# Attention on TensorE in row bands of 32: scores in bands 0 and 1, maxima in bands 2 and 3, keys and queries kept twice

## What is computed

```python
q = split_heads(layernorm(x) @ Wq + bq)          # 8 heads of 4 numbers, 2048 queries
k = split_heads(ctx @ Wk + bk)                   # 1601 keys
v = split_heads(ctx @ Wv + bv)
attn = softmax(q @ k.T / sqrt(32))               # 8 x 2048 x 1601
x = x + tanh(g_xattn) * (merge_heads(attn @ v) @ Wo + bo)
xf = layernorm(x)
scores = softmax(xf @ router_w + router_b)       # 8 experts
G, idx = top_k(scores.T, 512)                    # each expert takes its 512 best tokens
eo = relu(xf[idx] @ w1 + b1) @ w2 + b2
x = x + tanh(g_ffn) * scatter_add(eo * G)
```

## Time and profile before

| | before |
|---|---|
| median of 3 runs (lowest, highest) | 595.6 us (595.19, 595.64) |
| profiled execution: its time | 594.75 us |
| profiled execution: its span | 592.9 us |
| TensorE matmul busy | 551.4 us, 93% |
| VectorE busy | 444.1 us, 75% |
| ScalarE busy | 397.4 us, 67% |

### The profile page before, as it was taken

How to read it: one execution, slowest core, us unless ns; L and a number is a source line. 1 busy time by engine, 2 the same in 40 slices (tenths; PEclk the granted TensorE clock), 3 DMA queues, 4 the chain that set the end, 5 groups by cost and what they waited for, 6 DMA issues and landing times.

```text
span 592.9 us, 12821 instructions
## 1 busy us (share of the span) xinstructions
PE 551.4 (93%) x5043; PEld 318.6 (54%) x5043; DVE 444.1 (75%) x811; ACT 397.4 (67%) x774; POOL 196.8 (33%) x193
## 2 busy tenths in 40 slices
PE   6798899998999989999999998899999999999994
PEld 4433333333333333333333344469889898898974
DVE  3889879996798967989897258746767868677541
ACT  2587789987888878898888830044665646655651
POOL 3058030024420063400158010240735626346234
PEclk9999999999999999999999999999999999999998
DMA  8600000000000000000000004122735556356133
GB/s 280 241 2 1 1 1 3 2 1 38 2 36 2 2 37 1 37 2 1 37 38 2 36 19 140 34 60 72 163 112 117 144 136 148 108 107 163 16 36 35
DMA packets 23807, 35.80 MB, mean 60 GB/s; under 512 B 3459, under 2 KB 16196, under 8 KB 23620
## 3 DMA queue, kind: packets, MB, share of 16 engines
q1 hardware_dynamic: 17604, 26.59, 13.8%
q0 software_dynamic: 6144, 8.39, 8.3%
HBM read 26.59 MB, written 8.39 MB: 59 GB/s over the span
## 4 chain that ended last, share of the span: by engine, by line
PE 67%; DVE 18%; ACT 5%; issue 4%; POOL 3%; DMA 1%; POOLq 0%; ACTq 0%; DVEq 0%; SPq 0%
PE ps L1719 15%; PE ps L1726 15%; PE ps L1488 12%; DVE mquart L1016 11%; PE ps L1475 6%; PE ps L1454 6%; PE ps L1384 2%; ACT probs L741 2%; PE ps L1345 2%; POOL xn L528 2%; PE ps L1360 1%; PE ps L1697 1%; PE ps L1672 1%; ACT osb L641 1%; PE ps L1513 1%
## 5 line engine op out<-in xcount | busy, mean ns | idle before, releaser
L1016 DVE TENSOR_REDUCE mquart<-ps 128x2 f32<-128x802 f32 x256 | 241.9, 988 | 33.4 <-PE ps L1454 30.2
L741 ACT ACTIVATE probs<-ps 128x512 f32<-128x512 f32 (+1 forms) x416 | 222.9, 599 | 24.0 <-PE ps L1475 20.8
L1488 PE MATMUL ps<-probs,vp 128*32 128x256 f32 (+1 forms) x1664 | 132.7, 391 | 4.5 <-ACT osb L641 4.5
L1454 PE MATMUL ps<-kpad,qrows 64*128 64x401 bf16 x512 | 90.6, 337 | 3.7 <-DVE mquart L1016 3.1
L1475 PE MATMUL ps<-qfull,kpad 64*128 64x256 bf16 (+1 forms) x832 | 89.8, 272 | 2.8 <-ACT x L762 0.9
L1313 DVE TENSOR_TENSOR h1l<-hf,h1h 128x512 fp32r<-128x512 f32 x64 | 44.4, 693 | 56.0 <-ACT hf L868 56.0
L867 ACT ACTIVATE h1h<-ps,b1T 128x512 fp32r<-128x512 f32 x64 | 44.0, 687 | 53.8 <-PE ps L1719 53.6
L1726 PE MATMUL ps<-w2h,h1h 128*128 128x256 f32 x256 | 73.8, 288 | 2.2 <-DVE h1l L1313 1.5
L1726 PE MATMUL ps<-w2l,h1h 128*128 128x256 f32 x256 | 72.4, 283 | 0.0
L1726 PE MATMUL ps<-w2h,h1l 128*128 128x256 f32 x256 | 72.3, 283 | 0.0
L1475 PEld LDWEIGHTS ps<-qfull,kpad 64*128 64x128 bf16 (+1 forms) x832 | 38.9, 96 | 48.2 <-ACT probs L741 25.1
(11 more groups left out here) (198 smaller groups left out, 682.3 us busy)
## 6 DMA issues: line engine op xcount, KB each, us to landing
w1raw<-in_L_ffn_w SPq DMA_DIRECT2D x16, 512.0 KB, 4.6
w2raw<-in_L_ffn_w SPq DMA_DIRECT2D x16, 512.0 KB, 4.7
xs<-in_x SPq DMA_DIRECT2D x4, 512.0 KB, 7.7
ctx_sb<-in_ctx SPq DMA_DIRECT2D x3, 512.0 KB, 5.8
out<-xs SPq DMA_DIRECT2D x3, 512.0 KB, 2.6
x_rows<-x SPq DMA_DIRECT2D x3, 512.0 KB, 2.6
b2b<-in_L_ffn_b SPq DMA_DIRECT2D x1, 1024.0 KB, 11.1
out<-xs SPq DMA_DIRECT2D x2, 256.0 KB, 2.0
```

Source lines behind the costliest of these rows:

```text
L741: nc.scalar.activation(out_p, ps[0:w, next_bank(), :], ACT.Exp, scale=float(SCALE)).then_inc(s_ex, 1)
L1016: nc.vector.tensor_reduce(mquart[:, u % 2, t, a, :, kq], ps[:, b:b + 2, 0:MAXW], AX.X, ALU.max).then_inc(s_mr, 1)
L1454: last = mm(ps[:, bank + b, 0:MAXW], qrows[band(b), g, q:q + P], kpad[band(b), g, a, lo:lo + MAXW], start=True, stop=True)
L1488: last = mm(ps[32 * hh:32 * hh + 32, PV, 0:UW], vp[0:w, kt, g, hh, :], probs[0:w, step % PROBS, hh, :], start=(kt == 0), stop=(kt == NKT - 1))
```

## The change

Keys are no longer padded. `kbands` holds each head's keys once in its own 32 rows, and `kturned` holds the same with partitions 0 to 63 and 64 to 127 exchanged, by DMA from `kbands`. The queries of a chunk are copied the same way from partitions 0 to 63 to 64 to 127 of `qturned`. Each score matmul and each maximum matmul now has 32 rows: scores use partitions 0 to 31 and 32 to 63 (`score_band`), maxima 64 to 95 and 96 to 127 (`max_band`). `qfull` has two halves `v` on partitions 0 to 63: `v` 0 for the two heads that stand there, `v` 1 for the two that stand in the other half, with 64-column matmuls in `place_max` and a 64x512 copy in `q_full`. In a step the `v` 0 scores of both banks come first, then the first tile, then the `v` 1 scores, then the second tile. The heads stand on the partitions in another order (`place_of`), for which the weights are spread anew with ten copies in place of eighteen. The SyncE queue gets 16 transfers for the keys and 8 for the queries; the bias `b2b` and the first expert weights stand behind those of chunk 0, and the loop of the stores is written out.

```diff
-        kpad = ar("kpad", [P, NG, 2, KEYS], BF16)
+        kbands = ar("kbands", [P, NG, KEYS], BF16)
+        kturned = ar("kturned", [P, NG, KEYS], BF16)
...
+            def turn_keys(j, g):
+                lo, w = KB[j]
+                sp.wait_ge(s_rows, BLOCKS.index(("k", j, g)) + 1)
+                sp.dma_start(kturned[64:P, g, lo:lo + w], kbands[0:64, g, lo:lo + w]).then_inc(s_kup[g], 16)
+                sp.dma_start(kturned[0:64, g, lo:lo + w], kbands[64:P, g, lo:lo + w]).then_inc(s_kdown[g], 16)
+            def turn_queries(c, g):
+                sp.wait_ge(s_rows, rows_of(c, g))
+                if c > 1:
+                    sp.wait_ge(s_mm, TILES * (PER_CHUNK * (c - 2) + PARTS * (g + 1)))
+                sp.dma_start(qturned[64:P, g, c % 2, :], qrows[0:64, g, CW * c:CW * c + CW]).then_inc(s_qt[NG * (c % 2) + g], 16)
...
-                take(qfull[:, g, UW * h:UW * h + UW], ps[:, next_bank(), 0:UW], s_qf)
+                take(qfull[0:64, g, :, UW * h:UW * h + UW], ps[0:64, next_bank(), :].rearrange("p (v q) -> p v q", v=2), s_qf)
...
-                split(j, j % 2, w, 2, krows[:, j % 2, 0:w])
-                dve.wait_ge(s_rows, j + 1)
-                for b in range(2):
-                    last = nc.vector.tensor_scalar(kpad[:, 0, b, lo:lo + w], krows[:, j % 2, 0:w],
-                                                   cst[:, C_HEAD + b:C_HEAD + b + 1], None, ALU.mult)
-                last.then_inc(s_kpad0, 1)
+                split(j, j % 2, w, 2, kbands[:, 0, lo:lo + w])
...
                 for b in range(2):
-                    last = mm(ps[:, bank + b, 0:MAXW], qrows[band(b), g, q:q + P], kpad[band(b), g, a, lo:lo + MAXW], start=True, stop=True)
+                    rows = max_band(b)
+                    queries = qrows[rows, g, CW * c + q:CW * c + q + P] if a else qturned[rows, g, c % 2, q:q + P]
+                    keys = (kbands if a else kturned)[rows, g, lo:lo + MAXW]
+                    last = mm(ps[:, bank + b, 0:MAXW], queries, keys, start=True, stop=True)
...
-                mm(ps[:, bank, 0:UW], ident_bf[:, :], qrows[:, g, q:q + UW], start=True, stop=False, skip_group_check=True)
+                for v in range(2):
+                    mm(ps[0:64, bank, UW * v:UW * v + UW], ident_bf[:, 64 * v:64 * v + 64], qrows[:, g, q:q + UW],
+                       start=(v == 0), stop=False, skip_group_check=True)
...
                 for kt in range(NKT):
+                    first, second = score_bank(u, kt, 0), score_bank(u, kt, 1)
+                    scores(u, kt, 0, 0, first)
+                    scores(u, kt, 1, 0, second)
                     for n in range(tiles_by(u, 2 * kt - 1), tiles_by(u, 2 * kt)):
                         max_tile(n)
-                    scores(u, kt, 0)
-                    scores(u, kt, 1)
+                    scores(u, kt, 0, 1, first).then_inc(s_sc, 1)
+                    scores(u, kt, 1, 1, second).then_inc(s_sc, 1)
```

More of the change, by code:

```diff
@@ L338, in dve_bank, with score_band, max_band, place_of @@
             return 3 + 2 * (n % 2)
[L340 to L342 removed]
+        def score_band(p):
+            return slice(32 * p, 32 * p + 32)
+        def max_band(b):
+            return slice(64 + 32 * b, 64 + 32 * b + 32)
+        def place_of(head):
+            return 2 * (head % 2) + head // 2
         PLACE = 10
@@ L431, in _ @@
                 load_w2(0, half)
-            with sp.Fori(0, LAST) as c:
+            for g in range(NG):
+                turn_queries(1, g)
+            for c in range(LAST):
                 sp.wait_ge(s_x1, c + 1)
-                sp.dma_start(out_v[:, bass.ts(c, CT), :], xs[:, bass.ts(c, CT), :]).then_inc(s_out1, 16)
+                sp.dma_start(out_v[:, CT * c:CT * c + CT, :], xs[:, CT * c:CT * c + CT, :]).then_inc(s_out1, 16)
+                if c + 2 < NC:
+                    for g in range(NG):
+                        turn_queries(c + 2, g)
                 sp.wait_ge(s_x2, c + 1)
-                sp.dma_start(x2_v[:, bass.ts(c, CT), :], x2[:, :, :]).then_inc(s_x2st, 16)
+                sp.dma_start(x2_v[:, CT * c:CT * c + CT, :], x2[:, :, :]).then_inc(s_x2st, 16)
             for half in range(2):
@@ L907, in _, with heads @@
-            for j in range(2):
-                for g in range(NG):
-                    last = nc.vector.tensor_copy(
-                        bqkr[:, NG * j + g, :].rearrange("p (h j d) -> p h j d", h=HG, d=HD)[:, :, 0:6, :],
-                        bias_sb[:, 32 * j + 16 * g:32 * j + 16 * g + 16].rearrange("p (h d) -> p h d", d=HD).unsqueeze(2).to_broadcast([1, HG, 6, HD]))
+            def heads(a, x):
+                return a.rearrange("p n (y x d) -> p n y x d", x=2, d=HD)[:, :, :, x, :]
@@ new lines, in places @@
+            def places(a, x):
+                return a.rearrange("p n (x y j d) -> p n x y j d", x=2, y=2, d=HD)[:, :, x, :, :, :]
+            w_in, w_out = [t[:, :, :].rearrange("p k (g c) -> p (k g) c", g=NG) for t in (wk_sb, wq_sb, wv_sb)], [
+                t[:, :, :, :].rearrange("p k g r -> p (k g) r") for t in (wkr, wqr)]
+            b_in = bias_sb[:, :].rearrange("p (n c) -> p n c", c=16)
+            for x in range(2):
+                for src, dst in zip(w_in, w_out):
+                    nc.vector.tensor_copy(places(dst, x)[:, :, :, 0:6, :], heads(src, x).unsqueeze(3).to_broadcast([P, KD * NG, 2, 6, HD]))
+                nc.vector.tensor_copy(places(w_out[0], x)[:, :, :, 7, :], heads(w_in[2], x))
+                nc.vector.tensor_copy(places(bqkr[:, NG:2 * NG, :], x)[:, :, :, 7, :], heads(b_in[:, 2 * NG:3 * NG, :], x))
+                last = nc.vector.tensor_copy(places(bqkr[:, :, :], x)[:, :, :, 0:6, :],
+                                             heads(b_in, x)[:, 0:2 * NG].unsqueeze(3).to_broadcast([1, 2 * NG, 2, 6, HD]))
@@ L1462, in place_max, with scores, score_bank @@
                 bank = next_act((s_qf, u + 1))
-                mm(ps[:, bank, 0:UW], ident_bf[:, :], qrows[:, g, q:q + UW], start=True, stop=False, skip_group_check=True)
-                for t in range(UQ):
-                    last = mm(ps[:, bank, P * t:P * t + P], mparts[:, t, :, :].rearrange("p h r -> p (h r)"), ident_bf[:, :],
-                              start=False, stop=True, skip_group_check=True)
+                for v in range(2):
+                    mm(ps[0:64, bank, UW * v:UW * v + UW], ident_bf[:, 64 * v:64 * v + 64], qrows[:, g, q:q + UW],
+                       start=(v == 0), stop=False, skip_group_check=True)
+                    for t in range(UQ):
+                        last = mm(ps[0:64, bank, UW * v + P * t:UW * v + P * t + P], mparts[:, t, 2 * v:2 * v + 2, :].rearrange("p h r -> p (h r)"),
+                                  ident_bf[:, :], start=False, stop=True, skip_group_check=True)
                 last.then_inc(s_mpl, 1)
-            def scores(u, kt, p):
+            def scores(u, kt, p, v, bank):
                 c, g, h, r = unit(u)
                 w = kt_rows(kt)
-                bank = next_act((s_ex, 2 * (NKT * u + kt) + p + 1))
-                for b in range(2):
-                    last = mm(ps[0:w, bank, UW * b:UW * b + UW], kpad[band(p), g, b, P * kt:P * kt + w],
-                              qfull[band(p), g, UW * h:UW * h + UW], start=True, stop=True)
-                last.then_inc(s_sc, 1)
+                if (c, h, kt, p, v) == (0, 0, 0, 0, 1):
+                    pe.wait_ge(s_kdown[g], 64)
+                rows = score_band(p)
+                return mm(ps[0:w, bank, UW * v:UW * v + UW], (kturned if v else kbands)[rows, g, P * kt:P * kt + w],
+                          qfull[rows, g, v, UW * h:UW * h + UW], start=True, stop=True)
+            def score_bank(u, kt, p):
+                return next_act((s_ex, 2 * (NKT * u + kt) + p + 1))
             def pv(u, kt):
```

62 lines of the change are left out of this document (21 added, 41 removed).

## The result

The changed kernel takes 607.9 us (median of 4 runs, 605.33 to 614.90), the kernel before in the same comparison 595.4 (594.61 to 595.64): 1.020 times as long, interval 1.014 to 1.026. Faster by 7 us was forecast; it is slower by 12.5. The profiled execution took 605.59 us with a span of 603.8. Its granted clock was 0.987 of full; 605.33 us came at 0.987 as well, 610.16 at 0.979 and 614.90 at 0.967. The kernel before held 0.992 to 0.997 in all 52 runs beside the experiments.

What follows compares the result with a forecast made beforehand. TensorE was taken as nearest to full in most attention units, VectorE as the bound in units r=3. Gains of 4.0, 5.4 and 0.3 us less 2.4 for placing gave 587.4, or 588.3 us as median, range about 584 to 592.

Steps and rivals of the forecast that it cites:

- part 1: Attention steps, scores beside maxima: 22 two-tile steps gain 4.0 us, 30 steps with other work gain 5.4 us.
- one-tile step: Attention step with one maxima tile: 1.09 us on the chain before, to stay at about 1.07, no gain taken.
- the sum: Whole kernel: -4.0 - 5.4 + 2.4 - 0.3 = -7.3 us, on a profiled 594.75 us.
- Placing: Maxima placed with more columns streamed: 2.4 us on TensorE over 11 placements; ScalarE's copy grows from 386 to 598 ns.
- the prologue: Ahead of the attention: fewer padding copies gain 0.7 us, first placement and copy cost 0.22 + 0.21; together -0.3 us.
- two-tile step: Attention step with two maxima tiles: to fall from 1.24 to 1.06 us, 0.18 each, 22 counted, 4.0 us.
- a granted clock of 1.2 GHz in the attention: Sign that the prediction is wrong: TensorE's clock at 1.2 GHz, against full 2.4 GHz, somewhere in the attention.
- that rival: In attention steps, 32-row matmuls don't run beside one another, scores' second pair waits for the tile; +13 us, 609; chance 0.09.
- The maxima starve: Attention tile stands behind both score banks' wait, TensorE late by 0.17 us in some 65 steps; costs 11, 599; chance 0.13.
- its sign: The reduction's idle time on VectorE, 30.7 us over the attention before, grows.

Runs made afterwards that it cites:

- experiment 6: Changed kernel's order, but the second bank's wait moved behind the first bank's first score matmul; 604.7 us (598.55 to 606.79).
- Experiment 5: Bands of 32 rows and the old matmul order, but both banks' waits put ahead of everything in a step; 609.6 us (608.83 to 615.94).
- experiment 2: Changed kernel's bands of 32 rows, with the step order and waits of the kernel before; 595.3 us (591.88 to 603.43, 10 runs), ratio 0.999.
- experiment 4: Kernel before, with the maxima placed twice into one bank and ScalarE's copy 128x512, only half used; 597.9 us, +2.5 us.
- fourth kernel of experiment 7: Bands of 32, old order and waits, filler matmuls only ahead of the wait for GpSimd's rows; 592.1 us (591.19 to 604.84, 10 runs), ratio 0.9954.
- experiment 7: Four kernels with filler matmuls added to hold TensorE's clock, three in the old order, one in the changed kernel's; 594.2, 611.0, 594.6 and 592.1 us.
- two lower heaps of experiment 7: Runs of its first kernel (old order, fillers in three places): 592.0 to 592.1 us at clock 0.995, and 593.5 to 594.4 at 0.992.
- experiment 1: Kernel before (64 rows, padded keys) with only the changed kernel's order and waits in a step; 616.2 us, 1.035 times the kernel before.
- third kernel of experiment 7: Bands of 32, old order, fillers in unit 0's first four steps, ahead of GpSimd's wait and output projection, small ones in the last unit; 594.6 us.
- the first, second and fourth kernel of experiment 7: First: old order with bands, fillers in three places, 594.2 us. Second: same fillers in the changed kernel, 611.0. Fourth: fillers only ahead of GpSimd's wait, 592.1.

## Why the prediction was wrong

The prediction had 588.3 us; the kernel takes 607.9. Four kernels, with and without bands and in either order: the units r=1, 2 and 3 of chunk 1 at full clock, and the last unit's plain step:

| | r=1 | r=2 | r=3 | plain step |
|---|---|---|---|---|
| before | 20.87 | 18.16 | 15.51 | 0.98 |
| bands, old order | 20.40 | 17.55 | 15.23 | 0.98 |
| new order, no bands | 22.31 | 19.76 | 16.87 | 1.15 |
| changed kernel | 21.34 | 19.00 | 15.88 | 1.15 |

**The step that failed is the exponential's loop in part 1.** I saw the joint wait and added up the loop it makes, 0.04 + 0.11 + 0.27 + 0.04 + 0.60 = 1.06 us, and concluded that it hardly bites because a one-tile step takes 1.07 already. It measured 1.15. Narrow windows of the trace have every piece of it, beside the score matmuls at 347.80 and 347.91 shown above:

```profile
347.06 0.60 ACT L760 ACTIVATE probs<-ps 128x512 f32<-128x512 f32 x1
347.77 0.09 PEld L1496 LDWEIGHTS ps<-qfull,kbands 32*128 32x128 bf16 x1 [0.64 <-ACT probs L760]
348.21 0.60 ACT L760 ACTIVATE probs<-ps 128x512 f32<-128x512 f32 x1
```

The exponential ends at 347.66, the first score matmul starts at 347.80, the second pair at 347.91, the next exponential at 348.21: 0.60 + 0.14 + 0.11 + 0.30 = 1.15. All pieces are as I had them but one: from the exponential's end to the first score matmul it is 0.14, where I had put 0.04 from a row in which the values' single wait is met. (The bracket of 0.19 at that matmul counts from the end of the values, a little earlier.) In the changed kernel two waits for ScalarE are together ahead of one matmul; in experiment 6, where each has a matmul of its own, the same hand-over takes 0.05, 340.94 to 340.99. Of the 0.14, 0.11 lie ahead of the weight load and 0.03 between the load and its matmul. That two waits on one matmul are the reason is what this difference suggests; no run shows why they take that long.

With the loop at 1.15, the 17% above the 0.98 of a plain step are paid in all steps that nothing else bounds, and no slack is left to catch up after ScalarE's or TensorE's other work. I also took 1.07 as what a one-tile step is; the last unit in the trace before would have told that the engines can go faster than that and use it to catch up. There ScalarE has eight exponentials without a gap, two for each step, and the values of the first two of these steps start at 336.38 and 337.36, 0.98 us apart:

```profile
336.38 4.14 ACT L741 ACTIVATE probs<-ps 128x512 f32<-128x512 f32 x8
```

Experiment 5 has the joint wait with the old order and loses 13 us to experiment 2 at nearly the same clock; experiment 2 has the waits and the order of before, and gains 12.5 on the changed kernel. Not all of that is the loop. Experiment 6 has no loop above 0.98 us and is still 5 to 7 us above experiment 2 at like clock; so the loop is about half of it, by this difference, and the rest is what experiment 6 shares with the changed kernel, every tile behind a wait for ScalarE above all.

**The rest of the sum held in its costs, not in its gain.** Placing is 2.5 us by experiment 4 (forecast 2.4). The first reduction starts at 28.49 us, 0.8 earlier (forecast 0.7), the exponentials at 47.8 in place of 48.2 (the prediction had 0.3 us). The copy to `qfull` takes 591 ns. The turned keys land after 2.0 us. The gain is smaller than I had it, even with the loop gone. Units r=1 and r=2 were to be shorter by 1 to 1.5 us; in experiment 2 they are by 0.47 and 0.61. Over the whole kernel my estimate, from the best run of the fourth kernel of experiment 7 (591.2 at 0.995, against 595.3) with the 2.5 of placing added back, is 6.6 us with the prologue, where the sum had 9.7. Nor does it come from where I had it. I gave one-tile steps without other work nothing; they fall, one in unit r=2 of chunk 1 from 1.07 us (values at 170.67 and 171.74 before) to 0.90 (169.57 and 170.47 in experiment 2). I gave each two-tile step 0.18; of that unit's three, one falls from 1.23 to 1.05 and two get longer, from 1.24 to 1.42 and from 1.25 to 1.31.

**The clock is the term that was not in the sum.** I wrote that a granted clock of 1.2 GHz in the attention would prove me wrong and gave it neither a price nor a chance. Over the changed kernel's four runs the time goes with it, from 605.33 us at 0.987 to 614.90 at 0.967. A fall of 3.4 us costs about 1 us where its unit can be compared (23.47 against 22.44); at half clock no more than half its length of TensorE's work is lost, so the 2.1 us between the two lower heaps of experiment 7 are not one such fall alone, and what else they are stays open. The long fall costs about 10 (604.0 against 594.2, where the profiled execution has a short one beside it). What brings the falls is not shown: experiment 1 has them without bands, and before the change there are stretches with TensorE less busy and no fall. What is shown is that of the profiled executions the kernel before and experiment 4 have none in the attention, and that every other one but that of the third kernel of experiment 7 has.

So the balance is: the order with its joint wait 12.5 us (experiment 2 against the changed kernel), about half of it the loop; and in experiment 2, which ends level with the kernel before, placing 2.5 and about 4 for the clock (its median of 595.3 against the 591.2 above, an estimate, since the fillers differ too), against a gain from the bands and the prologue of 6 to 7. These don't add exactly, since a wait and a fall can hide one another.

**The rivals.** That bands of 32 run side by side, which I gave 0.91, is what the chip does; the sum of that rival was also off, 595.6 + 13 + 2.4 being 611 and not 609. "The maxima starve" is in part right. VectorE's idle time grew by 8.4 us, its sign, and the 5 to 7 us that remain in experiment 6 are its kind of loss, where the rival had 11; no run splits them between the tile's place and the rest of the order. It has no part in the plain steps, which have no tile and show the loop. The rule of the Trainium skill that I weighed ("TensorE: Matmul & The Clock Gate", section "Part 3: Packing small matmuls", starts in program order) fails with bands of 32 as it did with 64: in experiment 2 the queue holds both matmuls of the first bank, then both of the second, and they start as two pairs across the banks, 332.48 and 332.58 (each row here stands for one matmul of each bank):

```profile
332.48 0.27 PE L1496 MATMUL ps<-qfull,kbands 32*128 32x256 bf16 x2
332.58 0.27 PE L1496 MATMUL ps<-qfull,kturned 32*128 32x256 bf16 x2
```

So the interleaving by hand was not needed: the engine does it from the old order, as long as the waits let it.

## What to carry to other kernels

When two waits are joined, write down the loop that the later one closes, from a row in which that very hand-over happens, with every piece between the releasing instruction's end and the first result; compare it with the fastest step the trace has, not with the usual one. Keep a wait directly ahead of the first instruction that needs it: TensorE brings matmuls on other row bands forward by itself. Give the clock a price and a chance when work moves on TensorE: here its falls cost about 4 us of a gain of 6 to 7. Fillers where TensorE waited for another engine anyway cost nothing (22.27 us for a unit with eight, 22.29 without); 256 columns in each step of the last unit cost 1.2 us.

## What was not expected of the hardware

- In the last unit, kernels with score matmuls of 32 rows had a fall of the clock of 27.3 us with TensorE busy throughout. Three profiled executions show it (the first, second and fourth kernel of experiment 7); by their granted clocks of 0.963 to 0.969 one more run of the first and of the fourth, and one of experiment 2, probably had it. No run of the kernel before did. Why the same program holds the clock in most runs stays open.
- TensorE kept full clock with 1.96 us of matmuls in 3.4 us (before the change) and lost it behind 2.9 in 3.4.
- Moving one wait by one matmul, over instructions of 0.11 us, changed a plain step from 1.15 to 0.98 us.
- A pair of score matmuls, a pair of tile matmuls and the next scores of 32 rows each started within 0.12 us of one another and took 0.27 to 0.34 us each as they do alone: no cost was seen of four bands writing to four banks.
